# First expert layer: 36 packed tiles of 128 slots in place of 48 tiles of 96, with all gathers issued ahead of all stores

## What is computed

```python
logits = x @ gate_weight.T
logits = jnp.where(old_to_new[None, :] == -1, -jnp.inf, logits)
probs = jax.nn.softmax(logits.astype(jnp.float32), axis=-1)
top_v, top_i = jax.lax.top_k(probs, TOP_K)
top_v = top_v / jnp.sum(top_v, axis=-1, keepdims=True)
flat_e = old_to_new[top_i].reshape(-1)
pos = jnp.sum(jnp.cumsum(oh, axis=0) * oh, axis=-1) - 1      # oh: one-hot of flat_e
valid = pos < CAP                                            # CAP = 96
xb = jnp.zeros((E, CAP + 1, H)).at[flat_e, pos_c].set(x[tok])[:, :CAP]
g, u = jnp.split(jnp.einsum('ech,eoh->eco', xb, gate_up_proj), 2, axis=-1)
out = jnp.einsum('eci,ehi->ech', jax.nn.silu(g) * u, down_proj)
y = out[flat_e, jnp.minimum(pos_c, CAP - 1)]
final = jnp.zeros_like(x).at[tok].add(y * w[:, None])        # w: top_v where valid
```

## Time and profile before

| what | value |
|---|---|
| median of 3 runs | 1965.68 us (1964.38 to 1971.95) |
| the profiled execution's own time | 1977.1 us |
| its span in the trace | 1975.4 us |
| mean granted PE clock over the span | 0.887 of full speed |
| busy over the span | PE 79%, DVE 60%, ACT 43%, POOL 38% |

### The profile page before, as it was taken

One profiled execution on the slowest core, in us unless ns is written; L12 is line 12 of the kernel. 1 busy time (PEld: TensorE's weight loads), 2 busy tenths in 40 slices (PEclk: granted clock), 3 DMA queues, 4 the chain that ended last, 5 costly groups with the idle time before them and its releaser, 6 DMA issues. The chain is left out here.

```text
span 1975.4 us, 39043 instructions
## 1 busy us (share of the span) xinstructions
PE 1556.2 (79%) x14365; PEld 1083.4 (55%) x14365; DVE 1185.5 (60%) x2439; ACT 850.1 (43%) x2334; POOL 757.2 (38%) x1069
## 2 busy tenths in 40 slices
PE   5878961575025689899999988999899998857998
PEld 2433441454012467667766766777577666744555
DVE  6774139321745577687767776787677775323444
ACT  2225830121014465565566556656565664311111
POOL 6001000576001455466456655565554565310000
PEclk9998985688557799899999998999899999858999
DMA  6000010364422434554465356445634643111111
GB/s 218 1 2 2 1 60 15 108 201 123 170 54 74 127 95 124 145 138 126 111 159 136 114 126 165 116 124 140 163 103 108 171 123 106 39 33 40 32 40 45
DMA packets 227797, 196.37 MB, mean 99 GB/s; under 512 B 87459, under 2 KB 204067, under 8 KB 225568
## 3 DMA queue, kind: packets, MB, share of 16 engines
q1 hardware_dynamic: 218656, 180.35, 33.3%
q0 software_dynamic: 4608, 9.44, 1.6%
q10 hardware_dynamic: 4352, 4.20, 0.6%
HBM read 121.79 MB, written 72.03 MB: 98 GB/s over the span
## 5 line engine op out<-in xcount | busy, mean ns | idle before, releaser
L1468 PE MATMUL d_big<-all_xn_t,d_w 128*128 128x512 f32 x512 | 278.5, 672 | 57.4 <-DVE d_conv L1679 41.8
L1679 DVE SCALAR_TENSOR_TENSOR d_conv<-d_big,d_cw,d_conv 128x1023 f32<-128x1023 f32 (+2 forms) x192 | 245.8, 1280 | 68.6 <-ACT d_conv L1843 65.2
L2029 POOL TENSOR_TENSOR d_y<-d_y,all_xn 128x256 f32<-128x256 f32 x128 | 105.1, 821 | 186.4 <-DVE d_y L1822 130.3
L1468 PEld LDWEIGHTS d_big<-all_xn_t,d_w 128*128 128x128 f32 x512 | 96.3, 208 | 140.4 <-issue 97.2
L1943 ACT COPY d_ys<-d_big 128x128 f32<-128x128 f32 x256 | 63.0, 264 | 201.7 <-PE d_big L1613 201.6
L1651 PE MATMUL d_big<-d_wo,d_yt 128*128 128x256 f32 x512 | 129.6, 400 | 14.6 <-DVE d_yt L1749 14.6
L2218 PE MATMUL e_gu<-all_xn_t,e_up_w 128*128 128x512 f32 x272 | 121.9, 602 | 15.3 <-DMA e_dn_w<-in_L_ffn_Wd 15.3
L1584 PE MATMUL d_big<-d_w,all_xn_t 128*128 128x256 f32 x512 | 129.2, 398 | 0.1
L1843 ACT ACTIVATE d_conv<-d_big,d_cw 128x1024 f32<-128x1024 f32 x64 | 71.4, 1116 | 133.0 <-PE d_big L1468 114.7
L1723 DVE SCALAR_TENSOR_TENSOR d_AI<-d_big,d_b_col,d_decay 128x256 f32<-128x256 f32 x256 | 105.3, 474 | 38.8 <-PE d_big L1481 37.9
L1986 POOL TENSOR_TENSOR d_vs<-d_vs,d_sv 128x1024 f32<-128x1024 f32 x32 | 61.2, 1912 | 168.1 <-DMA d_vs<-turned_v_scratch 166.8
(11 more groups left out here) (330 smaller groups left out, 3776.3 us busy)
## 6 DMA issues: line engine op xcount, KB each, us to landing
turned_kq_scratch<-d_turned SPq DMA_DIRECT2D x32, 512.0 KB, 7.6
d_kq_tok<-turned_kq_scratch SPq DMA_DIRECT2D x128, 128.0 KB
turned_v_scratch<-d_vs SPq DMA_DIRECT2D x16, 1024.0 KB, 4.3
d_vs<-turned_v_scratch SPq DMA_DIRECT2D x64, 256.0 KB
grouped_y_scratch<-d_yx SPq DMA_DIRECT2D x32, 512.0 KB, 3.4
d_yx<-grouped_y_scratch SPq DMA_DIRECT2D x128, 128.0 KB
d_w<-in_L_attn_W_qkvz SPq DMA_DIRECT2D x16, 768.0 KB
l_gu<-in_L_ffn_gate_up_proj SPq DMA_DIRECT2D x48, 192.0 KB, 2.9
```

What stands on the lines that cost most here:

```text
L1468: mm = pe.matmul(big[0][:, c, :], w_sb[par][:, k, n * DK:(n + 1) * DK], xn_t[:, k, c * 512:(c + 1) * 512], start=(k == 0), stop=(k == KD - 1))
L1679: dve.scalar_tensor_tensor(conv[:, sh:T], src[:, 0:T - sh], cw[:, bass.ds(g, 1), COLUMN_OF[j], 3 - sh], conv[:, sh:T], ALU.mult, ALU.add). ...
L2029: pool.tensor_tensor(part, part, zs[:, t, :], ALU.mult).then_inc(s["yg_s"], 1)
```

## The change

Slots are packed across experts. Slot number 96·e + position, from 0 to 4607, is divided into 36 tiles of 128 rows, so a tile holds rows of two neighbouring experts and three tiles hold four experts. DVE computes the slot number in the router and splits it into a tile number and a row; the one-hot tiles become 36 and 128 wide in place of 48 and 96. In the expert phase a gather, a pair of transposes, a copy out of PSUM and a store each serve a tile of 128 rows. `up`, silu and the product stay one for each expert. `down` writes an expert's rows into the tiles that they belong to, in pieces.

There is now a row buffer and a result buffer for each of the 36 tiles, and weights have 16 buffers in place of 8. POOL issues 2 gathers in the router phase, the other 34 at the start of the expert phase, and then the 36 stores.

The diff, cut to its core:

```diff
-EB = 8
+EW = 16
+NTILE = EK * CAP // P
+AHEAD = NTILE
+EARLY = 2
+QUAD = 4
+QB0 = 32
+NONE = 1 << 14
...
-        self.xe = [m.sb(f"xe{i}", [CAP, D]) for i in range(EB)]
-        self.gu = [m.sb(f"gu{i}", [P, KD, 2 * INTER]) for i in range(EB)]
-        self.dn = [m.sb(f"dn{i}", [INTER, D]) for i in range(EB)]
-        self.tok = m.sb("tok", [CAP, EK], I32)
-        self.place = m.sb("place", [CAP, EK], I32)
-        self.got = [m.sem(f"got{i}") for i in range(EB)]
-        self.loaded = [m.sem(f"loaded{i}") for i in range(EB)]
+        self.xe = [m.sb(f"xe{i}", [P, D]) for i in range(NTILE)]
+        self.gu = [m.sb(f"gu{i}", [P, KD, 2 * INTER]) for i in range(EW)]
+        self.dn = [m.sb(f"dn{i}", [INTER, D]) for i in range(EW)]
+        self.tok = m.sb("tok", [P, NTILE], I32)
+        self.place = m.sb("place", [P, NTILE], I32)
+        self.got = [m.sem(f"got{i}") for i in range(NTILE)]
+        self.loaded = [m.sem(f"loaded{i}") for i in range(EW)]
...
-    def rows_in(self, pool, e, xn_dram):
-
-        pool.indirect_dma_start(self.xe[e % EB][:, :], None, xn_dram,
-                                bass.IndirectOffsetOnAxis(ap=self.tok[:, e:e + 1], axis=0)).then_inc(self.got[e % EB], 16)
+    def rows_in(self, pool, j, xn_dram):
+
+        pool.indirect_dma_start(self.xe[j][:, :], None, xn_dram,
+                                bass.IndirectOffsetOnAxis(ap=self.tok[:, j:j + 1], axis=0)).then_inc(self.got[j], 16)
...
-            for e in range(EB):
+            for e in range(EW):
...
             pool.wait_ge(tok_s, 1)
-            for e in range(EB):
-                buffers.rows_in(pool, e, xn_dram)
+            for j in range(EARLY):
+                buffers.rows_in(pool, j, xn_dram)
...
-            then(dve.tensor_copy(pos_b[:, :, :], pos_f[:, :, :]))
+            then(dve.tensor_scalar(over[:, :, :], pos_f[:, :, :], float(CAP), float(NONE), ALU.is_ge, ALU.mult))
+            then(dve.scalar_tensor_tensor(slot_f[:, :, :], new_f[:, :, :], float(CAP), pos_f[:, :, :], ALU.mult, ALU.add))
+            then(dve.scalar_tensor_tensor(slot_f[:, :, :], slot_f[:, :, :], float(-CAP), over[:, :, :], ALU.add, ALU.add))
+            then(dve.tensor_copy(slot_i[:, :, :], slot_f[:, :, :]))
+            dve.tensor_scalar(at_i[:, :, :], slot_i[:, :, :], 7, None, ALU.arith_shift_right).then_inc(v, 1)
+            n += 1
+            then(dve.tensor_scalar(slot_i[:, :, :], slot_i[:, :, :], P - 1, None, ALU.bitwise_and))
+            dve.tensor_copy(tile_b[:, :, :], at_i[:, :, :]).then_inc(v, 1)
+            n += 1
+            then(dve.tensor_copy(row_b[:, :, :], slot_i[:, :, :]))
             for t in range(TT):
-                dve.tensor_tensor(hot_e[:, t, :, :], iota_b[:, 1:EK + 1].unsqueeze(1).broadcast_to([P, TOPK, EK]),
-                                  new_b[:, t, :].unsqueeze(2).broadcast_to([P, TOPK, EK]), ALU.is_equal).then_inc(hot_s, 1)
-                dve.tensor_tensor(hot_c[:, t, :, :], iota_b[:, 0:CAP].unsqueeze(1).broadcast_to([P, TOPK, CAP]),
-                                  pos_b[:, t, :].unsqueeze(2).broadcast_to([P, TOPK, CAP]), ALU.is_equal).then_inc(hot_s, 1)
+                dve.tensor_tensor(hot_e[:, t, :, :], iota_b[:, 0:NTILE].unsqueeze(1).broadcast_to([P, TOPK, NTILE]),
+                                  tile_b[:, t, :].unsqueeze(2).broadcast_to([P, TOPK, NTILE]), ALU.is_equal).then_inc(hot_s, 1)
+                dve.tensor_tensor(hot_c[:, t, :, :], iota_b[:, :].unsqueeze(1).broadcast_to([P, TOPK, P]),
+                                  row_b[:, t, :].unsqueeze(2).broadcast_to([P, TOPK, P]), ALU.is_equal).then_inc(hot_s, 1)
...
-        ye = [m.sb(f"ye{i}", [CAP, D]) for i in range(EB)]
-        xt_ps = [m.ps(f"xt_ps{i}", [P, KD, CAP]) for i in range(2)]
-        gu_ps = [m.ps(f"gu_ps{i}", [INTER, 2, CAP]) for i in range(2)]
-        y_ps = [m.ps(f"y_ps{i}", [CAP, D]) for i in range(2)]
-        sent = [m.sem(f"sent{i}") for i in range(EB)]
+        ye = [m.sb(f"ye{i}", [P, D]) for i in range(AHEAD)]
+        xt_ps = [m.ps(f"xt_ps{i}", [P, 512]) for i in range(2)]
+        gu_ps = [m.ps(f"gu_ps{i}", [INTER, 512]) for i in range(2)]
+        y_ps = [m.ps(f"y_ps{i}", [P, 512]) for i in range(3)]
+        sent = [m.sem(f"sent{i}") for i in range(AHEAD)]
...
+        def pieces(e):
+
+            at, end = CAP * e, CAP * e + CAP
+            while at < end:
+                n = min(P - at % P, end - at)
+                n = QB0 if at % P == QB0 else n
+                yield at // P, at % P, at - CAP * e, n
+                at += n
...
-            for e in range(EB, EK):
-                sp.wait_ge(y_mm, e - EB + 1)
+            for e in range(EW, EK):
+                sp.wait_ge(y_mm, e - EW + 1)
                 buffers.weights_in(sp, e, gu_t, down_t)
 
         @block.gpsimd
         def _(pool):
+            for j in range(EARLY, AHEAD):
+                buffers.rows_in(pool, j, xn_dram)
             pool.wait_ge(cleared, 16)
-            for e in range(EK):
-                pool.wait_ge(y_c, e + 1)
-                pool.indirect_dma_start(y_dram, bass.IndirectOffsetOnAxis(ap=buffers.place[:, e:e + 1], axis=0),
-                                        ye[e % EB][:, :], None, bounds_check=T * TOPK - 1,
-                                        oob_is_err=False).then_inc(sent[e % EB], 16)
-                if e + EB < EK:
-                    pool.wait_ge(xt_mm, e + 1)
-                    buffers.rows_in(pool, e + EB, xn_dram)
-            for j in range(EB):
-                pool.wait_ge(sent[j], 16 * EK // EB)
+            for j in range(NTILE):
+                if j + AHEAD < NTILE:
+                    buffers.rows_in(pool, j + AHEAD, xn_dram)
+                pool.wait_ge(y_c, j + 1)
+                pool.indirect_dma_start(y_dram, bass.IndirectOffsetOnAxis(ap=buffers.place[:, j:j + 1], axis=0),
+                                        ye[j % AHEAD][:, :], None, bounds_check=T * TOPK - 1,
+                                        oob_is_err=False).then_inc(sent[j % AHEAD], 16)
+            for i in range(AHEAD):
+                pool.wait_ge(sent[i], 16 * NTILE // AHEAD)
 
         @block.tensor
         def _(pe):
-            def turn(e):
-                pe.wait_ge(got[e % EB], 16 * (e // EB) + 16)
-                if e >= 2:
-                    pe.wait_ge(xt_c, e - 1)
+            def turn(j):
+                pe.wait_ge(got[j], 16)
+                if j >= 2:
+                    pe.wait_ge(xt_c, j - 1)
...
             def down(e):
                 pe.wait_ge(h_s, e + 1)
-                if e >= 2:
-                    pe.wait_ge(y_c, e - 1)
-                pe.matmul(y_ps[e % 2][:, :], h[e % 2][:, :], dn[e % EB][:, :], start=True, stop=True).then_inc(y_mm, 1)
-
-            turn(0)
+                for j, row, c, n in pieces(e):
+                    if j >= 3:
+                        pe.wait_ge(y_c, j - 2)
+                    mm = pe.matmul(y_ps[j % 3][row:row + n, 0:D], h[e % 2][:, c:c + n], dn[e % EW][:, :], start=True, stop=True,
+                                   skip_group_check=True)
+                mm.then_inc(y_mm, 1)
+
+            turned = 0
             for e in range(EK):
-                if e + 1 < EK:
-                    turn(e + 1)
+                while turned <= min(last_tile(e + 1), NTILE - 1):
+                    turn(turned)
+                    turned += 1
...
-            def keep(e):
-                act.wait_ge(y_mm, e + 1)
-                if e >= EB:
-                    act.wait_ge(sent[e % EB], 16 * (e // EB))
-                act.copy(ye[e % EB][:, :], y_ps[e % 2][:, :]).then_inc(y_c, 1)
-
+                act.activation(act_g[e % 2][:, :], gu_ps[e % 2][:, 0:CAP], ACT.Silu).then_inc(silu_s, 1)
+
+            def keep(j):
+                act.wait_ge(y_mm, last_expert(j) + 1)
+                if j >= AHEAD:
+                    act.wait_ge(sent[j % AHEAD], 16 * (j // AHEAD))
+                act.copy(ye[j % AHEAD][:, :], y_ps[j % 3][:, 0:D]).then_inc(y_c, 1)
```

84 lines of the change are left out of this document (49 added, 35 removed).

## The result

| kernel | median, us | runs, us | profiled execution: own time / span | granted clock |
|---|---|---|---|---|
| before | 1968.79 | 4, 1964.38 to 1971.95 | 1977.1 / 1975.4 | 0.887 |
| after | 1941.01 | 4, 1934.63 to 1944.75 | 1942.52 / 1940.5 | 0.899 |

The ratio is 0.9857, interval 0.982 to 0.9894. The forecast was 1942.8, between 1929 and 1956; it started from 1965.68, the median of before's first three runs.

The account below looks back on a forecast made before the run. The prediction took POOL's count of indirect DMAs to bound the expert phase. Its last store, moved by router, early gathers and list from 484.72 to 461.8, gave 1965.7 - 22.9 = 1942.8 us, range 1929 to 1956.

Parts of the forecast that it names:

- step 3: POOL's indirect DMA of 128 rows: bounded by 0.92 and 1.23 us, middle 1.07 taken, pitch 1.38.
- step 5: PE in the expert phase: pitch 1.82 us an expert, copy and store through at 456.8, 5 us ahead of POOL's list.
- first sign of being wrong: Stores in the expert phase that wait for ACT's `keep` would mean that PE is the bound.
- sign of being right: In POOL's trace, the mean of one indirect DMA would be near 1.07 us.
- Router arithmetic: DVE in the router: eight small operations in place of two and changed one-hot tiles cost +2.1 us, bounds 1.3 and 4.5.
- Two gathers ahead of the barrier: POOL at the router's end: two early gathers in place of eight save 7.35 us ahead of PE's start.
- 70 DMAs in place of 88 and the end of POOL's list: Expert phase: POOL's last store ends at 461.8 in place of 484.72, -22.9 us, without the start's wait of 9.2.
- Rows cost nothing: Rival on POOL's indirect DMAs: price stays 0.92 us for 128 rows, total 1932.0 us; chance 0.27.
- PE becomes the bound: Rival: changes between wide and narrow stationary tiles slow PE; fully, 1966.8, chance 0.07; in part or DMA engines, 0.10.
- Weights and results with more buffers: Expert phase: weights with 16 buffers and results with 36 change the time by 0.
- Behind the phase: Landing, drain and barrier after the last store keep their 9.65 us, change 0; 1.4 saved if drain follows DMA count.
- The DMA engines fall behind: Rival: gathers and weights ask 257 GB/s in the first 47 us, costing some 5 us, 1948; chance 0.10 with PE in part.

Follow-up runs that it names:

- f2: Changed kernel with 8 gathers ahead of the barrier in place of 2, run again on the third chip: 1974.84 us, ratio 0.9921 to the kernel before.
- e6: Changed kernel with ten more gathers of 16 to 128 rows, into buffers nobody reads, between its gathers and stores: 2002.17 us, a single execution.
- e1: Changed kernel with one full-width `down` matmul for each expert in place of the pieces, output not the reference's: 1930.49 us, ratio 0.9797 to the kernel before.
- e3: Kernel before with only the new order: 48 tiles of 96 rows, 2 early gathers, 46 gathers, then 48 stores, own buffers: 1965.46 us, ratio 0.9971.
- e2: Changed kernel with each `down` piece zero-padded to 128 stationary columns and summed in PSUM, 6 matmuls for 4 experts: 1935.34 us, ratio 0.9845 to before.
- f0: The changed kernel itself, with nothing altered, run again on the third chip: 1978.15 us, ratio 0.9943 to the kernel before.
- f1: Changed kernel with gathers 12 tiles ahead, then gather and store in turn, on the third chip: 1961.36 us, ratio 0.9839 to the kernel before.
- e5_early8: Changed kernel with 8 gathers ahead of the barrier in place of 2, on the second chip: 1979.89 us, ratio 0.9925 to the kernel before.

## Why the prediction was right

Point by point, by its own steps. The number was right in part by luck. The forecast phase, 102.6, is the length of POOL's list; the measured one, 103.5, is the length of PE's. POOL's list was forecast 8 us too long (step 3), and PE, which should have been 5 us ahead of it, came 6 us later than forecast (step 5) and set the end. The prediction's own first sign of being wrong, stores that wait for ACT's `keep`, is there: 11 of 36. Its sign of being right, a mean near 1.07 for one indirect DMA, is not.

1. *Router arithmetic.* Forecast +2.1, bounds 1.3 to 4.5. Memset to first gather went from 72.27 to 72.88, +0.6: below the lower bound. (The upper bound adds up to 4.4, not 4.5.) It is the difference of two single executions, but small either way.

2. *Two gathers ahead of the barrier, -7.35.* Right. The drain ended at 365.92, 1.94 behind the second gather (363.98), as it had ended 1.93 behind the eighth. From the first gather to PE's start went from 369.66 - 357.10 = 12.56 to 366.96 - 361.50 = 5.46, which is -7.1. The 0.8 us by which POOL was to start behind PE stood on no row; it was 367.56 - 366.96 = 0.60. f2 shows the same edge from the other side: with 8 early gathers PE's wait was 15.5, with 2 it is 7.7 or 7.8.

3. *Price of an indirect DMA with 128 rows.* **This term was mis-sized.** I took the middle between 0.92 and 1.23, 1.07. It is 0.944 for a gather and 0.982 for a store; e6 gives 0.001 us a row. I had the two signs of a large fixed part in front of me (gather and store alike, the first one longer) and still took the middle. 70 DMAs at 0.11 too much are 8 us. The Trainium skill's sentence in DMA: Bandwidth & Descriptors, section Anatomy of one DMA, that descriptor generation is small and many can be emitted before the cost shows, agrees with e6: 112 more rows cost 0.11 us. The 0.83 us that don't go with the rows are not in it.

4. *70 DMAs in place of 88 and the end of POOL's list.* The mechanism is right: with PE out of the way (e1) the phase is 94.9, and without the packing (e3) 121.0. The list behind the barrier is 88.3 long and not 96.3. The phase was forecast as 461.8 - 359.2 = 102.6 and came to 103.5, because the next step filled what this one freed.

5. *PE.* **That PE stays ahead of POOL's list is the step that failed.** Forecast pitch 1.82, with 0.10 for a change of width, and PE's end 5 us ahead of POOL's. Measured pitch 1.91, and 0.13 a change; PE's last matmul ended at 462.2, only 2.8 us ahead of the last store's end where 7 were forecast, and the stores waited for its results. Here the other term was a little too small: 44 x 0.09 = 4 us, and 1.5 more by the fifth expert (378.0 - 361.5 = 16.5 behind the first gather, 15.0 forecast). "PE has cover up to a pitch of 1.93" was right for a list of 1.38 a DMA. By the prediction's own numbers the cheap price, 0.92, ends POOL's list at 451.0 and leaves cover only up to (451.0 - 2.5 - 374.2)/44 = 1.69, less than its own 1.82: the rival *Rows cost nothing* had to give PE's 456.8 and some 1937.8 us, not 1932.0, and the two rivals belonged together. So *PE becomes the bound* came true in part. Its price was written down as up to a matmul's latency, 0.39 a change; e2 against after shows 0.13. The Trainium skill's rule in TensorEngine Tiling (Array Packing), Key Properties, that switching the tiling mode drains TensorE, agrees in its sign with the 0.38 us for three changes; whether these widths change that mode, no trace shows. The thought that two pieces might overlap in the array was wrong: two narrow pieces took longer (1.12) than two full ones (0.89).

6. *Weights and results with more buffers, 0.* Right: PE waited once, for 0.6 us, for rows, and never for weights.

7. *Behind the phase.* I left it open whether the drain goes with the number of DMAs or with their rows, and took 0. It goes with the number of indirect DMAs in that block, -1.3 us in the table. Shown by five counts (last part).

8. *The sum.* Router, phase, and what lies behind it: +2.1 - 25.0 + 0 = -22.9 was forecast, +0.6 - 24.1 - 1.3 = -24.8 came, by the traces of the two first executions. The rest of the difference between the two medians (27.8) is within what the kernel before alone moves between runs (1964.38 to 1971.95).

*The DMA engines fall behind* did not come: the share is 0.62 in 366 to 466, and no gather was late.

What the prediction had no place for: the size of the gain depends on the chip. On the first it was 25 us by the medians, on the third 15 us, with a trace in which the phase lasts 142.5 and is longer than the one of before elsewhere. Whether the kernel before has late starts there, I can't say; its median is 26 us higher there, so something costs it time too.

## What to carry to other kernels

Where POOL issues indirect DMAs back to back, count instructions, not rows: fill each to its 128 rows, and change the order only for what waits in it: with the tiles of 96 rows, gathers first bought 6.6 us of the phase, and with the packed tiles on the third chip it was slower than alternating (f0 against f1). Packing across units moves the cost to whoever has to cut at the tile borders: sum that engine anew, with a price for each change between narrow and full stationary tiles, and try zero padding with sums in PSUM before narrow pieces. And when a term is bounded from both sides, look which end the rows lean to before taking the middle: two errors of opposite sign gave a good number here, and only the waits in the trace after showed it. Then ask whether the other engines keep up at that end too.

## What the hardware showed that I had not expected

*The drain at the end of the expert block counts POOL's indirect DMAs.* Five kernels, all of whose results have landed:

| indirect DMAs in the block | kernel | drain, ns | ns for each |
|---|---|---|---|
| 64 | e5_early8 | 5282 | 82.5 |
| 70 | after | 5772 | 82.5 |
| 80 | e6_row_prices | 6583 | 82.3 |
| 88 | before | 7236 | 82.2 |
| 94 | e3_unpacked | 7726 | 82.2 |

```profile
L810 POOLq DRAIN  x1: 5282/5282/5282, 502.1 to 502.1; - x1
```

```profile
L794 POOLq DRAIN  x1: 7726/7726/7726, 479.9 to 479.9; - x1
```

Rows don't matter (88 and 94 are of 96 rows, 64 and 70 of 128, and 80 has eight smaller ones), and while it lasts the DMA engines move nothing (share 0.00 from 467 to 473). What it works at, no run here shows. At the end of the router's block, where POOL doesn't wait for landings first, the number hardly shows: the drain ended 1.93 us behind the last of 8 gathers in before, 1.94 behind the last of 2 in after, 2.1 behind the last of 8 in e5.

*Late starts of ACT and DVE.* In seven traces from two chips, and in none of the seven others, PE's finished work was picked up late, by 2 to 5 us at a time where gathers and stores alternated and by up to 20 us where they didn't; in f0 PE's idle stretches come to 34 us. It is put down to "remote" or "issue", so the profile knows no releaser. The chips on which it shows are the ones on which the kernel before takes 1993 and not 1967 us. The cause stays open; in f0, at least, no load of instructions ended them (none from 384 to 434). A comparison of two kernels should be made on one chip, and a single trace isn't proof of a stall's cause until the unchanged kernel has been looked at beside it.
